# Mixture-of-experts kernel: the slots of experts 0 and 1 of the last two batches are scattered first, and the first tile's matmuls stand ahead of the last batch's ranks

## The reference: what is computed

```python
    x = x + _L0_xattn_ref(ctx_512, _layernorm(x, axis=-1), L0_xattn_Wq, L0_xattn_Wk, L0_xattn_gamma_raw)
    x = x + _L0_ffn_ref(_layernorm(x, axis=-1), L0_ffn_router_weight, L0_ffn_router_bias, L0_ffn_gate_up_proj, L0_ffn_gate_up_proj_bias, L0_ffn_down_proj, L0_ffn_down_proj_bias)
```

```python
        logits = x @ router_weight.T + router_bias
        top_val, top_idx = jax.lax.top_k(logits, TOP_K)
        top_val = jax.nn.softmax(top_val, axis=-1)
...
        gate = jnp.minimum(gate, LIMIT)
        up = jnp.clip(up, -LIMIT, LIMIT)
        glu = gate * jax.nn.sigmoid(gate * ALPHA)
        out = jnp.einsum('etd,edh->eth', (up + 1.0) * glu, down_proj) + down_proj_bias[:, None, :]
        out = out * router_scores.T[:, :, None]
```

## Time and profile before

| | us |
|---|---|
| three runs | 916.93, 920.1, 911.8 |
| their median | 916.93 |
| the profiled execution's own time | 909.35 |
| its span, first to last instruction | 907.6 |
| PE busy in the span | 769.7 (85%) |
| DVE busy | 595.0 (66%) |
| ACT busy | 403.3 (44%) |
| POOL busy | 311.8 (34%) |
| mean granted share of TensorE's clock | 0.899 |

### The profile page before, as it was taken

The page is one execution under the profiler, slowest core; times in us unless marked ns, Lnnn a source line. Parts: engine busy times, 40 slices in busy tenths (PEclk is TensorE's granted clock), DMA queues, the critical chain, the costliest instruction groups (busy, mean ns, idle before and its releaser), DMA issues.

```text
span 907.6 us, 16747 instructions
## 1 busy us (share of the span) xinstructions
PE 769.7 (85%) x3566; PEld 623.9 (69%) x3567; DVE 595.0 (66%) x1068; ACT 403.3 (44%) x663; POOL 311.8 (34%) x352
## 2 busy tenths in 40 slices
PE   4454726157799999999999999999999999999993
PEld 1134425145588888878888887887788878888882
DVE  4678948396584845775657768677757475776541
ACT  3999767612153423344343525434443243352221
POOL 1331626476323222333232322323333222333231
PEclk9675755556899999999999999999999999999997
DMA  8501111116574642654737465486547354723332
GB/s 281 194 0 48 47 43 51 47 48 197 120 188 96 186 95 49 205 143 132 208 67 219 114 165 161 105 228 181 166 130 208 74 130 137 214 57 58 56 58 32
DMA packets 70706, 112.06 MB, mean 123 GB/s; under 512 B 29894, under 2 KB 32198, under 8 KB 70598
## 3 DMA queue, kind: packets, MB, share of 16 engines
q1 hardware_dynamic: 32454, 74.22, 24.2%
q0 software_dynamic: 18416, 36.53, 20.7%
q10 hardware_dynamic: 19728, 0.15, 1.2%
HBM read 84.05 MB, written 28.90 MB: 124 GB/s over the span
## 4 chain that ended last, share of the span: by engine, by line
PE 71%; ACT 11%; DVE 5%; issue 5%; another core or an unknown queue 2%; POOL 2%; SPq 1%; DMA 1%; ACTq 1%; DVEq 1%; POOLq 0%
PE gate_up_ps L853 41%; PE bank L853 21%; PE bank L843 3%; PE bank L835 3%; ACT bgu L519 3%; ACT marks L519 3%; DMA bd_raw<-_ffn_down_proj_bias_dram 1%; ACT x_sb L532 1%; POOL step_u L413 1%; SPq L282 1%; ACT w L656 1%; ACT xn L550 1%; ACT A L529 1%; DVE hl L1038 1%
## 5 line engine op out<-in xcount | busy, mean ns | idle before, releaser
L853 PE MATMUL gate_up_ps<-w,xh 128*128 (+1 forms) x1152 | 364.9, 398 | 1.5 <-DVE xl L1033 1.5
L853 PEld LDWEIGHTS gate_up_ps<-w,xh 128*128 128x128 f32 x1152 | 213.0, 190 | 43.0 <-issue 1.9
L438 POOL DMA_INDIRECT out_dram<-yb,aslot x72 | 131.9, 1833 | 281.9 <-ACT yb L637 247.7
L853 PE MATMUL gate_up_ps<-w,xl 128*128 (+1 forms) x576 | 226.7, 394 | 0.0
L853 PE MATMUL bank<-w,hh 128*128 (+1 forms) x576 | 180.5, 395 | 7.4 <-DVE hl L1038 6.6
L630 ACT ACTIVATE sg<-gc 128x512 f32<-128x512 f32 x72 | 45.6, 634 | 226.0 <-DVE gc L1048 203.8
L429 POOL DMA_INDIRECT xg<-xn_rows,gslot x75 | 76.7, 1022 | 183.6 <-DMA gslot<-slot_rows 163.9
L1044 DVE TENSOR_TENSOR gu<-gate_up_ps,bgu 128x1024 f32<-128x1024 f32 x72 | 88.2, 1225 | 74.0 <-PE gate_up_ps L853 54.4
L853 PEld LDWEIGHTS bank<-w,hh 128*128 128x128 f32 x576 | 107.8, 189 | 36.1 <-issue 14.2
L1038 DVE TENSOR_TENSOR hl<-bank,hh 128x512 fp32r<-128x512 f32 x72 | 49.6, 689 | 117.6 <-ACT hh L624 108.9
L853 PEld LDWEIGHTS gate_up_ps<-w,xl 128*128 128x128 f32 x576 | 109.0, 189 | 23.7
(11 more groups left out here) (209 smaller groups left out, 794.2 us busy)
## 6 DMA issues: line engine op xcount, KB each, us to landing
raw_w<-_L_ffn_gate_up_proj_dram SPq DMA_DIRECT2D x64, 512.0 KB
raw_w<-in_L_ffn_down_proj_dram SPq DMA_DIRECT2D x64, 256.0 KB
bgu<-n_gate_up_proj_bias_dram SPq DMA_DIRECT2D x16, 512.0 KB
x_sb<-in_x_dram SPq DMA_DIRECT2D x4, 1024.0 KB, 11.4
xn_rows<-xn SPq DMA_DIRECT2D x4, 1024.0 KB
out_dram<-x_sb SPq DMA_DIRECT2D x4, 1024.0 KB
xg<-xn_rows,gslot POOLq DMA_INDIRECT x75
out_dram<-yb,aslot POOLq DMA_INDIRECT x72
```

What stands on the lines that cost most here:

```text
L438: pool.indirect_dma_start(out_v, bass.IndirectOffsetOnAxis(aslot[:, k, 0:1], 0), yb[:, k % 2, :], None, bounds_check=TOKENS - 1, oob_is_er ...
L853: last = nc.tensor.matmul(out_ps, lhs[:, rows], w[:, bass.ds(buf, 1), part, c, cols].rearrange("p a d -> p (a d)"), start=(m == 0), stop=( ...
```

## The change

Four things are done.

1. DVE also works out separate columns for the first experts: for expert 0 in batch 2, and for experts 0 and 1 in batch 3 (`first_i`, `first_pay`, 4 columns for each). POOL writes these with `scatter_first`, 4 scatters ahead of batch 2's sixteen and 8 ahead of batch 3's. A token that doesn't have the expert gets an index beyond the table and is left out by a bounds check; in the ordinary 16 columns the entries of those experts get such an index (`skip`). That makes 76 scatters in place of 64.
2. SP waits for batches 0 and 1 and for the 4 scatters of expert 0 in batch 2 before it loads the slots of tiles 0 to 3. Ten of batch 2's sixteen scatters stand behind the gathers of these tiles. For tiles 4 to 6 it waits for batch 3's first 8. Expert 1 is counted with at least 4 tiles, so that tiles up to 7 belong to experts 0 and 1; it has 7 anyway, so that the number of tiles stays 72. The rest of batch 3's scatters stand between the next gathers and adds (6, 5 and 5). ACT waits for all 64 ordinary scatters in its step 5.
3. `high_x(0, 0)` of ACT, `low_x(0, 0)` of DVE and tile 0's first six matmuls of PE stand ahead of batch 3's exponentials, one-hot and ranks.
4. SP issues the last quarter of expert 1's weights behind the slots of tiles 4 to 6.

The diff, without the new buffers and names and most of the unchanged lines:

```diff
-            def load_half(e, h, bias_at, trio=0, j=0):
+            def load_half(e, h, bias_at, trio=0, j=0, only=None):
...
+                    if only is not None and c % HALF != only:
+                        at += 32
+                        continue
...
-                    sp.wait_ge(S["scat"], 16 * RT * TOP_K * EARLY)
+                    sp.wait_ge(S["scat"], 16 * RT * TOP_K * (EARLY - 1))
+                    sp.wait_ge(S["first_2"], 16 * RT)
...
-            load_half(1, 1, 1)
+            load_half(1, 1, 1, only=0)
...
-            sp.wait_ge(S["scat"], 16 * RT * TOP_K * NB)
+            sp.wait_ge(S["first_3"], 16 * RT * 2)
...
+            load_half(1, 1, 1, only=1)
...
+                    within = {} if k < RT * TOP_K * (EARLY - 1) else dict(bounds_check=SLOTS - 1, oob_is_err=False)
...
-                                            payload[:, k, :], None).then_inc(S["scat"], 16)
+                                            payload[:, k, :], None, **within).then_inc(S["scat"], 16)
...
+            def scatter_first(ready, rows, done):
+                pool.wait_ge(S["first_done"], ready)
+                for i in rows:
+                    for r in range(RT):
+                        pool.indirect_dma_start(slot_d, bass.IndirectOffsetOnAxis(first_i[:, i, r:r + 1], 0),
+                                                first_pay[:, i, r, :], None, bounds_check=SLOTS - 1,
+                                                oob_is_err=False).then_inc(S[done], 16)
...
-            scatter(EARLY, NT * TOP_K)
+            scatter_first(1, (0,), "first_2")
+            scatter(EARLY, 6)
...
-            scatter(NB, NT * TOP_K)
+            scatter(EARLY, NT * TOP_K)
+            scatter_first(2, (1, 2), "first_3")
+            scatter(NB, 6)
...
+            gather(FROZEN, 0)
...
-            for T in range(1, FROZEN):
-                gather(T + 3, (T + 3) % UNROLL)
-                add(T - 1, T - 1)
+            add(0, 0)
+            scatter(NB, 5)
+            gather(FROZEN + 1, 1)
+            add(1, 1)
+            scatter(NB, 5)
+            gather(FROZEN + 2, 2)
+            add(2, 2)
...
+                    if isinstance(T, int) and T == FROZEN + 1:
+                        act.wait_ge(S["scat"], 16 * NT * TOP_K)
...
+            high_x(0, 0)
...
-            high_x(0, 0)
...
-            def product(out_ps, high, low, buf, cols):
+            def product(out_ps, high, low, buf, cols, amid=None):
...
+                    if c == HALF and amid is not None:
+                        amid()
...
-            def gate_up(T, k, half, buf):
+            def gate_up(T, k, half, buf, amid=None):
...
-                last = product(psG[k % 2][:, cols], xh[:, k % 2, :], xl[:, k % 2, :], buf, cols)
+                last = product(psG[k % 2][:, cols], xh[:, k % 2, :], xl[:, k % 2, :], buf, cols, amid)
...
-                gate_up(T, k, 0, buf)
+                gate_up(T, k, 0, buf, (lambda: rank(EARLY)) if known(T) else None)
...
+            for i, b in enumerate((EARLY - 1, EARLY, EARLY)):
+                V.tensor_copy(first_pay[:, i, :, 0], token_id[:, RT * b:RT * (b + 1)].bitcast(u32)).then_inc(S["dve_c"], 1)
...
+                if b == EARLY:
+                    low_x(0, 0)
...
+                ahead = max(0, b + 2 - EARLY)
+                at = slice(0, 1) if b < EARLY else slice(1, 3)
+                if ahead:
+                    send(V.tensor_scalar(skip[:], ek[:].rearrange("p r k -> p (r k)"), ahead - 0.5, FAR, ALU.is_lt, ALU.mult))
...
+                if ahead:
+                    link(V.tensor_tensor(first_v[:, :, :, 0:ahead], hot[:, :, :, 0:ahead],
+                                         score[:].unsqueeze(3).broadcast_to([P, RT, TOP_K, ahead]), ALU.mult))
+                    send(V.tensor_reduce(first_pay[:, at, :, 1].bitcast(fp32).rearrange("p e r -> p r e"),
+                                         first_v[:, :, :, 0:ahead].rearrange("p r k e -> p r e k"), AX.X, ALU.add))
...
+                if ahead:
+                    send(V.scalar_tensor_tensor(out=first_pos[:, :, 0:ahead], in0=onehot[:, :, 0:ahead], scalar=-FAR,
+                                                in1=pos[:, :, 0:ahead], op0=ALU.mult, op1=ALU.add))
...
+                if ahead:
+                    V.tensor_scalar(first_i[:, at, :].rearrange("p e r -> p r e"), first_pos[:, :, 0:ahead], FAR, None,
+                                    ALU.add).then_inc(S["first_done"], 1)
...
-                link(V.tensor_copy(slot_i[:, sl], posk[:].rearrange("p r k -> p (r k)")))
+                if ahead:
+                    link(V.tensor_tensor(slot_i[:, sl], posk[:].rearrange("p r k -> p (r k)"), skip[:], ALU.add))
+                else:
+                    link(V.tensor_copy(slot_i[:, sl], posk[:].rearrange("p r k -> p (r k)")))
...
-                if b == EARLY:
-                    low_x(0, 0)
...
+            link(V.tensor_scalar(til[:, 1:2], til[:, 1:2], float(SECOND), None, ALU.max))
```

More of the change, by code:

```diff
@@ L30 @@
 EARLY = NB - 1
-TILES = -(-(TOKENS * TOP_K // P + E - 1 + FROZEN) // UNROLL) * UNROLL
+SECOND = 4
+TILES = -(-(TOKENS * TOP_K // P + E - 1 + FROZEN + SECOND - 1) // UNROLL) * UNROLL
 SLOTS = E * TOKENS
+FAR = float(1 << 20)
 GU = 2 * D
@@ L108, in xattn_moe_kernel @@
         payload = sb("payload", [P, NT * TOP_K, 2], u32)
+        first_i = sb("first_i", [P, 3, RT], u32)
+        first_pay = sb("first_pay", [P, 3, RT, 2], u32)
+        first_pos = sb("first_pos", [P, RT, 2])
+        first_v = sb("first_v", [P, RT, TOP_K, 2])
+        skip = sb("skip", [P, RT * TOP_K])
         at = -(-nc.sbuf_base // 64) * 64
@@ L236, in xattn_moe_kernel @@
                      "rank_ps", "dense_done", "scT_ps", "scT_done", "bd_ps", "bo_done", "acc_out", "slots_done",
-                     "payload_done", "scat", "chain", "words_done", "cnt_read", "table_in", "table_done", "guess_done", "counted", "moved", "ok_done", "ok_ps",
+                     "payload_done", "scat", "first_done", "first_2", "first_3", "chain", "words_done", "cnt_read", "table_in", "table_done", "guess_done", "counted", "moved", "ok_done", "ok_ps",
                      "raw_in0", "raw_in1", "hi_done", "lo_done", "xT_ps", "xh_done", "xl_done", "gu_ps", "gu_read", "gc_done", "sg_done",
@@ L892, in step @@
                     down(T - 1, (k - 1) % UNROLL, field(pe, own, "buffer_before"))
-            rank(EARLY)
             tr_x(0, 0)
```

## The result

The changed kernel took 922.70 us (median of 12 runs, 919.5 to 924.1) against 914.64 us for the kernel before (median of 12, 911.3 to 920.1). The ratio is 1.0074, with a 95% interval of 1.0051 to 1.0098: slower by 0.7%. Forecast were 915.3 us and no change. The case that came true is rival 2, the late signal that grows with the run of scatters; it had given 922.4 us and a chance of 0.14. That 922.4 and 922.7 lie so close is partly luck: the rival added 5.5 us to a median of 916.93, and measured were 8.1 us on top of 914.64.

The account below looks back on a forecast made before the run. PE, busy 642.1 of 651.6 us from 245.4 on, was taken as the bound, so only that stretch's start could move: of 4.6 us won, DVE's queue left 1.6, giving 916.93 - 1.6 = 915.3 us; range 904 to 926.

Parts of the forecast that it names:

- rival 2: PE's signal for tile 0's gate comes 12.5 us late instead of 5.4: +5.5 us, 922.4 us; chance 0.14.
- Tile 0's tokens earlier: SP's slot loads at 195.3, first gather 197.9, tokens by 202.2; necessary for the next part, alone worth nothing.
- Tile 0 ahead of the ranks: Tile 0's matmuls begin at 209.5, 4.6 us before 214.18; six take 2.6 us, ranks end at 213.7.
- DVE's extra columns: Small DVE operations: 0.4 us in batch 2, 0.5 in batch 3; first_v and first_pay hidden in the wait for the ranks.
- What is late next: DVE's queue before tile 0's gate: done at 223.1 against 224.58, leaving 1.5 to 1.6 of the 4.6 us.
- The rest of the scatters: POOL's 24 scatters end at 233.5; gathers of tiles 5 and 6 come 9.5 to 9.8 us apart; hidden by slack.
- The price of a checked scatter: A bounds-checked scatter on POOL costs the plain pitch, 1.27 us, with 1.88 kept for the range.
- rival 3: A checked scatter costs what an add costs, 1.88 us, so gathers of tiles 4 to 6 come late: 924.4 us; chance 0.12.
- The late signal: PE's signal for tile 0's gate stays 5.4 us late: gate at 228.4, back-transposes 231.9 against 233.5.
- Rival 1: PE's signal for tile 0's gate comes in time and the clock holds: -9.6 us, 907.3 us; chance 0.24.

Follow-up runs that it names:

- a_wait_only: Changed kernel, POOL waiting on its own semaphore, met at once, behind scatters 5, 10, 14, 18 of the 24; ratio to before 1.0009, before at 883.45 us.
- a_eight_more: Changed kernel with eight more scatters, into a table nothing reads, so 32 in a row instead of 24; ratio to before 1.0213.
- b_gaps_all_2: Kernel before with a small POOL operation behind every fourth of its 64 scatters, in a comparison with holds; 905.22 us, ratio to before 0.9911.
- a_short_gaps: Changed kernel with a small POOL operation behind the 5th, 10th, 14th and 18th of its 24 scatters; 908.97 us, ratio to before 0.9971.
- a_wait_only_2: Changed kernel, POOL's own semaphore waits, met at once, behind scatters 5, 10, 14, 18 of the 24, measured again; ratio to before 1.0104.

## Why the prediction was wrong, point by point

- **Tile 0's tokens earlier: half right.** Forecast were slots loaded from 195.3, the first gather at 197.9 and the tokens by 202.2; it was 197.34, 203.98 and 207.9. Some 2 us of it lie ahead of the change: batch 1's scatters, which it doesn't touch, began at 152.25 instead of 150.49, and that start lies between 150.2 and 153.9 in the kernels of either kind here that show the holds. The rest is a wait that the step overlooked. SP's loads now go out right behind 1 MB of output rows:

```profile
196.85 0.38 SPq L339 DMA_DIRECT2D out_dram<-x_sb  x1
197.34 0.44 SPq L330 DMA_DIRECT2D gslot<-slot_rows  x1
```

  They took 6.6 us until the gather instead of the 2.6 of the earlier trace rows, where the rows had gone out 10 us ahead and the DMA share was 0.10; from 197 to 204 it is 0.51, at 154 GB/s. That the output rows are the cause is read from the order, not tried. The late gathers had a price that the step doesn't name: the run of 24 scatters stands behind them, began at 210.0 instead of 203.0, and ended at 240.9 instead of 233.5.
- **Tile 0 ahead of the ranks: right.** The late tokens cost nothing here, since ACT's `norm` ran until 209.8. 211.21 less those 2 us is 209.2 (209.5 forecast). The six matmuls took 2.9 us (2.6 forecast), and the ranks' end at 215.3 less 2 is 213.3 (213.7 forecast).
- **DVE's extra columns: right.** `first_v` and `first_pay` lie in the wait for the ranks, of which 0.72 is left; `dense_s` ends at 218.54, less 2 is 216.5 (217.35 forecast). PE waited 0.94 for it (1 to 2 forecast).
- **What is late next: failed in its size.** DVE was to be done at 223.1; it was at 230.78, since `xl` of tile 1 and all four additions waited for held signals. The step took over 3.65 us of work from a stretch where they had come in time.
- **The rest of the scatters: wrong, but hidden by the larger loss.** "9.5 to 9.8 us" between gathers were 10.6 and 10.7 in the changed kernel as run, and 10.8 and 12.0 in a_wait_only. The pitch had been read from the quiet stretch of the earlier trace rows; beside tiles, scatters took up to 2.14 and adds 2.11 us in a_wait_only instead of 0.96 and 1.585. In the changed kernel as run, the late start of the tiles left the gathers in time.
- **The price of a checked scatter: right.** Pitch 1.29, against 1.27 taken and 1.88 as the upper bound; rival 3 is out.
- **The late signal: the step that failed.** "I take it to stay at its size of 5.4 us." It was 13.4 us by DVE's wait and 20.3 by the matmul's end. The prediction had both numbers at hand, 5.4 and 12.5, and the pattern (each in a run of scatters), and then carried the size instead of asking what ends a hold. In batch 2 it ended 2.5 us behind the run. By that rule the forecast was 233.5 + 2.5 = 236.0 for the gate and 239.6 for the back-transposes, 6 us behind the 233.5 of before, near rival 2's +5.5. The other 8 us to the measured 247.70 are the end of the run, which came 7.4 us later than forecast, and 0.8 us more between that end and the gate.
- **Chances.** The range held the time. Rival 2 described what came (a signal that grows with the run), but priced it by batch 2's 12.5 us, not by the end of the run. Rival 1 (a signal in time) was described rightly as a state of affairs, but its price was not: without holds the early start is lost to the gathers.

## What to carry to other kernels

When a wait in a trace has no instruction near its end, ask what ends it, not how long it was, and line it up with what the other queues do at that moment. Long rows of small indirect DMAs on GpSimd deserve suspicion as soon as another engine waits for TensorE inside them: keep them short, or break them with a wait for the signal that matters (a small operation in between is not a sure break), and count what must be out by when, since each pause is paid at the next gather. An early start is worth only what the following deadlines can keep up with; take the durations of those from a stretch that is as busy as the one they will stand in.

## What the runs showed of the hardware

- While GpSimd issues scatters without a break, a semaphore update of TensorE can reach others up to 28.7 us after the matmul's listed end (a_eight_more: 222.1 to 250.84). The gate then starts mostly 1.4 to 3.6 us after the run's end, in some cases within it (229.97 in the kernel before, whose run ended at 233.8). In the traces with holds, runs of four or five with other work of POOL or a gap between them made the gate wait for 3 us at most, but ACT waited 6.29 and 6.63 us in one of them (b_gaps_all_2). One operation of 0.22 us in between, with 0.8 us behind it, let the gate's signal through (a_short_gaps); a semaphore wait without a gap didn't (a_wait_only_2), and an operation of 0.20 us with 0.28 us behind it didn't in batch 1 of b_gaps_all_2. Which part holds the update stays open. The Trainium skill ("Perfetto Trace Analysis", the section "Tensor Engine Instruction") says that a matmul's end in a trace is worked out from its size, and that its semaphore update follows once PSUM has acknowledged the writes. No run here shows at which of these points the delay arises.
- The kernel before ran for one whole comparison 3.4% faster than in the next (883.45 against 914.08 us); the traces of the first, of three kernels close to it, show no hold. No run tells what differs.
- A scatter beside DVE's `scalar_tensor_tensor` of 2.35 us took 2.71 us, one beside the weights' remainder (`tensor_tensor`, 3.43 us for two) 2.14, against 0.98. The first is from the changed kernel, the second from a_wait_only. The Trainium skill ("SBUF — State Buffer", "Who interferes with whom") says that a DVE operation with two inputs in SBUF contends with a GpSimd instruction that reads SBUF; both DVE operations have two such inputs, and the scatters take their indices from SBUF. If that makes a scatter such a reader, which is read from these rows and not tested, the traces agree. The prediction had looked at the page's rule for `tensor_scalar` alone. The rows:

```profile
188.48 2.35 DVE L1152 SCALAR_TENSOR_TENSOR x_sb<-A,gam,x_sb 128x2048 f32<-128x2048 f32 x1
...
188.97 2.71 POOL L407 DMA_INDIRECT slot_rows<-payload,slot_i  x1 [0.30 <-issue]
```
